# A two-layer decoder on one core: the written-out order of the steps on four engines is replaced, and 111 filler matmuls become 101

## What is computed

```python
x = _layernorm(x + _L0_attn_ref(x, ...))        # 7-wide windowed attention, 16 heads
x = _layernorm(x + _L0_xattn_ref(x, ctx, ...))  # attention to a context
x = _layernorm(x + _L0_ffn_ref(x, ...))         # 8 experts, 16 tokens each, own attention
x = _layernorm(x + _L1_attn_ref(x, ...))        # attention with a decay mask
x = _layernorm(x + _L1_xattn_ref(x, ctx, ...))  # argmax picks a context row, then 16 heads
x = _layernorm(x + _L1_ffn_ref(x, ...))         # ternary weights, 3-wide conv, silu, 1024 hidden
```

## Time and profile before

| | us |
|---|---|
| median of 3 runs | 997.79 (997.18 to 1002.22) |
| the profiled execution, its own time | 997.79 |
| its span | 996.0 |
| PE busy | 924.0 (93%) |
| DVE busy | 855.2 (86%) |
| ACT busy | 737.9 (74%) |
| POOL busy | 217.8 (22%) |

### The profile page before, as it was taken

One profiled execution on the slowest core, in us unless ns is written; L12 is line 12 of the kernel. 1 busy time (PEld: TensorE's weight loads), 2 busy tenths in 40 slices (PEclk: granted clock), 3 DMA queues, 4 the chain that ended last, 5 costly groups with the idle time before them and its releaser, 6 DMA issues.

```text
span 996.0 us, 20555 instructions
## 1 busy us (share of the span) xinstructions
PE 924.0 (93%) x7507; PEld 675.5 (68%) x7507; DVE 855.2 (86%) x2217; ACT 737.9 (74%) x1852; POOL 217.8 (22%) x469
## 2 busy tenths in 40 slices
PE   6888999999999999999999999999999999988887
...
DVE  5887576599999999999999999989999997877877
...
GB/s 277 374 94 74 85 30 66 11 86 1 61 57 62 55 13 105 19 99 1 117 1 44 74 22 96 12 106 2 116 2 43 64 23 1 22 12 12 12 1 22
DMA packets 36629, 59.08 MB, mean 59 GB/s; under 512 B 6656, under 2 KB 15872, under 8 KB 36016
## 3 DMA queue, kind: packets, MB, share of 16 engines
...
## 4 chain that ended last, share of the span: by engine, by line
PE 61%; ACT 16%; DVE 14%; POOL 4%; issue 3%; SPq 2%; DMA 1%; POOLq 0%; DVEq 0%; ACTq 0%
PE bank_c L505 17%; PE banks_e L505 8%; PE bank_a L505 7%; PE bank_x L505 7%; PE bank_f L505 4%; PE bank_x L716 4%; ACT area_e L1768 3%; DVE neg_top L1364 3%; PE bank_a L611 3%; ACT squares_out L1544 2%; PE banks_e L895 2%; DVE area_f L1442 2%; ACT x L1551 2%; ACT area_bx L1532 2%; PE bank_c L536 2%
## 5 line engine op out<-in xcount | busy, mean ns | idle before, releaser
L1442 DVE SCALAR_TENSOR_TENSOR area_f<-area_f,w_convw 128x254 f32<-128x254 f32 x240 | 104.7, 478 | 6.2 <-ACT area_f L1815 4.4
L1532 ACT ACTIVATE area_bx<-bank_x 128x512 f32<-128x512 f32 (+1 forms) x140 | 68.1, 499 | 23.9 <-PE bank_x L716 7.4
L1364 DVE TENSOR_REDUCE neg_top<-banks_e 128x8 f32<-128x1024 f32 x64 | 76.2, 1219 | 8.4 <-PE banks_e L505 8.1
L1213 DVE TENSOR_TENSOR area_a<-area_a 128x512 f32<-128x512 f32 x112 | 74.5, 683 | 1.0
L1158 DVE TENSOR_TENSOR area_a<-area_a 128x512 f32<-128x512 f32 x112 | 73.3, 683 | 2.4 <-PE bank_a L611 1.4
L1815 ACT ACTIVATE area_f<-area_f,w_convb,w_convw 128x256 f32<-128x256 f32 x120 | 65.4, 596 | 10.1 <-DVE area_f L1433 9.7
L1768 ACT ACTIVATE area_e<-banks_e 128x512 f32<-128x512 f32 x120 | 64.1, 602 | 8.4 <-PE banks_e L895 8.1
L1217 DVE TENSOR_TENSOR area_a<-area_a 128x512 f32<-128x512 f32 x96 | 65.7, 684 | 0.4
L1532 ACT ACTIVATE area_a<-bank_a 128x512 f32<-128x512 f32 (+1 forms) x80 | 44.0, 550 | 20.1 <-PE bank_a L505 14.6
L1532 ACT ACTIVATE area_bx<-bank_c 128x512 f32<-128x512 f32 x64 | 34.4, 537 | 26.8 <-PE bank_c L505 19.5
L1864 POOL TENSOR_TENSOR area_bx<-area_bx,minus 128x2 f32<-128x2 f32 x16 | 13.1, 819 | 180.0 <-ACT area_bx L1557 180.0
...
## 6 DMA issues: line engine op xcount, KB each, us to landing
...
```

What stands on the lines that cost most here:

```text
L1213: made[wi] = own.mark(dve.tensor_tensor(v4, v4, bc(e4[:, :, wi, :], 3, DH), ALU.mult))
L1364: dve.tensor_reduce(top[:, b, r:r + 2, :, 0].rearrange("p r (par c) -> p r c par", c=DC), banks_e[:, r:r + 2, :].rearrange("p r (c par k) ...
L1442: last = dve.scalar_tensor_tensor(c4[:, i, :, dst], h4[:, i, :, src], cwt3[:, 2 * jj + i, k:k + 1], c4[:, i, :, dst], ALU.mult, ALU.add)
L1532: return act.activation(dst, src, ACT.Copy)
```

## The change

`WARM` goes from 111 to 101, and the tables of PE, DVE, ACT and POOL are replaced. SP's table stays. No instruction other than the ten fillers is added or removed, no wait and no buffer is changed; each station's steps keep their order among themselves.

```diff
-WARM = 111
+WARM = 101
...
 ORDER = {
     "PE": (
-        "QQQASASSASBQSQBAQAASDABABSBBQBQXBXASAXQXAXABXBABYBYQBYYYQYBAYAXQCXCABXBXAXBAXBQYCYQCYYYBYCAYCAXBXQDAXDXD"
...
+        "QQQASSAASSBQQBSQAQADSBABASBBQBQXBXASAXQXAXABXBABYBYQBYYQYYBAYAXQCXCABXXBAXBAXBQYCYQCYYBYCAYCAXBXQDAXDXD"
...
     ),
```

More of the change, by code:

```diff
@@ L82 @@
-        "WWFWWWWHWWFWWFWWWWWHWWWWHWHHH"
+        "QQQASSAASSBQQBSAQAADSBABASBBQBQXBXASAXQXAXABXBABYBYQBYYQYYBAYAXQCXCABXXBAXBAXBQYCYQYCYYBYCAYCAXBXQDAXDXD"
+        "XDADXEBABYYEQBYCEBEQECYECEYCYECCAEYTDTDADXQDFAXDFDFABXEFBEXBFAXEBXEBFBYECQCEYCECQHYEYCEYHCYTDYTDXADHDADX"
+        "DFQEFBXFEXFBXBFEBEXFBACEBAYCAEYCQCEQYHEYCHYCEYDTYDTDHXADADXDFQEFBFEBAXBFXBXEFXBEBFAYCEYACQECYCEYQYHCECYD"
+        "EYDHTXDTDAHXADDQEFBFXEFBXBFXAEFBEFCXAACYEBBYECQCEYQYCHYEYECYTHDXTDHXDADADFDFQFXEBFEBXAFBEXBXFBAEBAYCEQCY"
@@ new lines @@
+        "ECYECYHEDHEYCYCYTQTDAHXADXDQFDFDAEXBFEBXFBEXBXBFAEBYEFCEAYCQCYQCYECHYCYDYEXEDHATDTDHDAXDQFEFBFXEFBXBABXF"
+        "BEXEFABECYECAYCYQCYHEYQCYEHCEYTDXTADHDXDADDFEFBFXEBXFBQBXFAEBXFEBAECYACYECYECYQHECYHCEYDQTDYDTXDHDAXDABE"
+        "FQFXEFBXBFEBXAFEBFXBAACECEYQCYECQYEYHCYEYTCTYDAXDHADXDHDQDAEFBFEXFBFXBABEXEFABBXCFEQEYCYECYCHYEYCEYTCYDX"
+        "HQDXTDHADADDFQXEFBFEFBXBABXBEFBEFCXEACAYECYECYYHDECYEHCYTBTYDHXDAXDFADFDFXFEXBEBXBXEBFBEYCCFEYECEYCYXYEY"
+        "CEHCTYHDTDXHDDFFDFXDFXCECXEFCCXFCECEYEDYEEYDYHDYHEYDEYDDHTTECCEFCFFCFEECFCEFDEDDEEDEHDTHDTWEHWWEWFWWFWFW"
@@ new lines @@
+        "CAAAAAAQQQQYCAAXXXXXXXXXXAADDDXYYYEEBBAAYYEEEEEEAAAAAAABAAAAAEEAAAAAACCCEQEYQQQTAAFFFDDDAAXXXXFXXXXXFXEE"
+        "FFEEEFEEEFFFBBFFYAYAYXBAAFFFFAFAEEFFFYAYFFCCAAHHAHAAAACEEAAAAAAYHHHHTQQQQHDDDFFFAXXAXXXXXXXEEFXEFEFFEEEE"
+        "FFFFBBFFFFYYYAABFFFXFYYAAEFAAEFAACFFAACAAHHHAAAACEEAAAHHHHYATAQAHFFFDDDAQQQAXXXXXEEXXFXXEEXEEFEFFEBBFFFF"
+        "XYAAYYBFFFFAAYYFFFFAAAFFEEACACAFFAAAAAACAAAAEHHEHYAHHHQHAQTDDQQDHFAFXAXFXXXXXXXEEXEFEFEEFFEFEFFFBXBFFAAF"
+        "FYYYFFAAFAABFAYYFFEEFCCAFAAAAAAAAHAHAHEAAECAYHHHHATHQQFFQFDDDXXAQXXXXXXXAFEEFFFXEEEEEEFFFFBFBAAFFYFXYYBA"
@@ new lines @@
+        "AFFFFFFYYEEAAAAAAFFCCAAHHHAAAAEAEAAACHHAHHAYTQQHQFAFQFADDXDXXXXXXXXAAEEFXEEEEEEFFFFBBFFFXYYYFFBFFAAFFFFY"
+        "YEEAAAAAFAFCCFFAAAACAAAAAHAYAHHAEEHHQQQHHTDDDQHAFXFFXXXXXXXXEEAFXEFFFEEFBEBEEFFFAAFFXFFYBYYFFFEEFAAYYFFA"
+        "AAAFFCAHCAHHAAAAAAAAACEEAYAHHAHHTQQQQHDDDXFFFXXXXXXXAXEEXFEEEAFFFEFBBEEFFFFFAYAFFBYYFXFFFAAYEYFEFAAAAAFF"
+        "CCAAHAHHHHCAEHHAEAAAAYAAAAQTDDDQQXXQXXXHAFXXFXFXEEAXEFEEEFEEFFBBFXFFFFAAFFBFAAYYYAAFFFAAFAEEAAAYYFFCCFFA"
+        "AAEEAAAACAHHHAAYQTHHHHAAQQQDDDXXFXXXHFXXXAFXEEAEFXEEEFEEFFBBFFFFAAFBFFYYYFFFEEFFFFYYAAAAFXAFCCAAAEEAAAAC"
@@ L101 @@
+        "HYHHAAAAAHHAHHXXQXTXXXHXXDDDFFFXAAQQQEEFEXEFFFFBBEEEEFFFXFBFFAAFFYYYFFFAAFFEEAYYFAFCCAHAAHHAAAEEHHCHHAAA"
+        "ATAAYAAAAHFFFDXDDXXXXXXAXXFXFEEFFXEEFEBEBEEFFYFYYBFFFFFEYEYFFFFFCCFFEEHHHCYHHHHTXXXXXHFFFDDDXXXXFXXFFFEF"
+        "EFEEEEFEEFCCFFFFFYFYYFCFFFYEEYFFHHHHHDEDDHHYETHEEFFFEEEEFEECCFFFFFCFFFFFFFFFFFFFFEEDEDEDHHHHHHHTEEHFFFEE"
+        "EEFEEFFFFFFFFFFFFFFFFFEEFEFEHHHHHTHHFFFHFFFFFFFFFFFFFFFFFFFFHHHHHHHHH"
     ),
     "ACT": (
-        "QQSQSSASSASBQBQASQAADSABSABBSSSSSBQSSBBSXQSXAABQXAXSBXSABBAYSSBYQYYBYBSQYSSBAYAYXQCXACBXBASXABXYQCBYYQYC"
```

57 lines of the change are left out of this document (18 added, 39 removed).

## The result

The changed kernel takes 1013.73 us (median of 4 runs, 1013.01 to 1014.0), the kernel before beside it 999.5 us (997.18 to 1002.22, 4 runs): a ratio of 1.0139, with a 95% interval of 1.0112 to 1.0166. The prediction was 1001.9 us with a range of 989 to 1009. The time lies outside it. The profiled execution of the changed kernel took 1010.35 us, and its span is 1008.4 us: 12.4 more than before, where the sum said 4.1. It is the shortest of the six executions on record and has the highest mean granted clock, 0.991 (the other five took 1012.94 to 1014.0 us at 0.985 to 0.989).

The account below looks back on a forecast made before the run. PE was taken to set the pace, busy 97% from 200 to 850 us. Span 996.0 + 1.0 + 3.9 - 0.8 = 1000.1 us, plus 1.8 around the span, gave 1001.9 us, range 989 to 1009.

Parts of the forecast that it names:

- The end of E15: Last group, on DVE: group 14's convolution and other instructions now stand before and between E15's, sliding its end by +3.9 us.
- The middle: 200 to 850 us: the new order taken as nothing, bounded by 10 us of gain and 6 us of loss.
- neighbours of one bank: PE's table, middle: two steps of one bank with nothing between, 12 before and 13 now, 0.5 us each on average.
- the middle gets worse: Rival, PE from 200 to 850 us: ten or twelve more short waits, +5 to +6 us, 1007 us; chance 0.14.
- D15's queries: On ACT near the end: the copy `chosen_q` starts later behind more exponentials and a copy, +1.0 us.
- H14 out of the last stretch: On DVE, 966 to 987 us: H14's addition moves in front of F15's first L1433, -0.8 us.
- Fillers: Last stretch on PE: ten fillers fewer cost nothing, as they stand where PE would be waiting anyway.
- The clock rival: Last stretch: fewer fillers let PE's clock fall in H15's pairs, 1.4 us later, 1003.3 us; chance 0.12.

Follow-up runs that it names:

- part4: The kernel before with the new order only from T14's addition (934 us) to the end, 101 fillers; ratio 1.0054 to the kernel before.
- tail_old: The changed kernel up to T14, from there the old order with its 111 fillers; ratio 1.0098 to the kernel before, span 1005.1 us.
- swaps: The changed kernel with another step put between adjacent steps of one chain, on PE alone, in five places from 834 to 917 us; ratio 1.024 to the kernel before.
- part3b: The kernel before with the new order only from X14's addition (847 us) to T14 (934 us); ratio 1.0025 to the kernel before, span 998.7 us.
- few_fillers: The kernel before with 22 fillers fewer behind F15's first step, 89 in all; ratio 1.0021 to the kernel before, span 998.8 us.
- act_d15: The changed kernel with D15's copy of the queries moved ahead of an L1824 and E14's copy, on ACT alone; ratio 1.0133 to the kernel before.

## Why the prediction was wrong, and where it was right

**The end of E15, +3.9: right in size and in mechanism.** The change makes 3.8 us between T14 and E15's addition; putting the new tail on the old front makes 3.8 too (part4), and putting the old tail on the new front takes it to 0.1 (tail_old).

**The middle, taken as nothing: the step that failed most.** Up to C13 the change loses 6.2 us, of them 2.5 by 758 us and 3.7 in the 87 us behind it. The prediction counted neighbours of one bank, 12 before and 13 now, at 0.5 us each, and found the difference too small to matter. The count was a sample of one cause of waits, and it was taken over the whole middle in one piece. By lines of the table it goes from 11 to 8 in the second to seventh and from 1 to 5 in the eighth, and the eighth, by its steps in the trace, covers about 745 to 850 us (the ninth what follows, not "800 to 900"). There the waits grew by five, and by 2.3 us, and those for ACT by 3.0. So the rise was in the tables, in the place where the time was lost. The rival "the middle gets worse" named the right place, PE waiting for copies, and its 5 to 6 us is nearly what came. Its price per wait is not confirmed: the stretch is 4.0 us longer with 2.3 us more of waits, and swaps, which took such pairs apart, only made others. Which letters do it I have not separated, so the cause inside the stretch stays open; that it is the order and not the clock, the traces show. (The prediction also took all of PE's idle time in the middle for waits for copies. Of its recorded waits there before, 18.7 us, 4.5 are for DVE.)

**From 850 to 934 us: a stretch that was left out of the sum.** The prediction took one detail from it, D15's queries, for +1.0, and treated it with the letters beside it. It is 2.4 us in the change and 2.6 alone (part3b), and 4.5 alone when the old order too has its full clock there. The detail was exact, 3.98 us between the two copies, and the sentence that went with it was wrong: the two L1815 "cost nothing as long as that idle time is there". It was not there, and in the old order it is there only where the clock falls. ACT in part4, with the old order at a granted clock of 1.00:

```profile
921.05 0.57 ACT L1532 ACTIVATE area_d<-bank_c 128x512 f32<-128x512 f32 x1
```

No idle time stands ahead of the copy; there PE waits 0.72 us for it. The 1.83 us of rows 4 are ACT waiting for PE's transposes, behind logits and a product that ran at half clock (2.02 us for 1.09). An idle time is a cover only if what makes it will be there again.

**H14 out of the last stretch, -0.8: 0.6 in part4, nothing in the change.** From the first L1433 to L1501 the kernel before takes 15.92 us, part4 with the new tail 15.35, so it gains 0.6. The changed kernel takes 15.89: at half clock the transposes at L977 take 1.06 to 1.11 us for 0.6, and DVE waits 0.59 for the last of them. It may be no gain of its own either: in the old order H14's L1511 come only behind E15's addition, so it seems to be E15's delay that makes room for it. No run tests that.

**Fillers, nothing: right where they only fill, wrong as a cover.** The clock rival, of 1.4 us in H15's product, came in part4 (1.3), few_fillers (1.1), act_d15 (1.8) and swaps (1.3), and in the change as the 0.5 us of the step above. The Trainium skill ("TensorE: Matmul & The Clock Gate", its section on a second HAM failure mode) says that many short idle times between groups of matmuls make the clock swing. These runs agree: PE is idle for 5.1 and 5.6 of the 21 us ahead of the product in few_fillers and part4 and for 2.3 in the kernel before, which has a clock of 1.00 up to 987 us and pairs 0.22 us apart in the product. The five slower executions of the change may have lost their 2.6 to 3.7 us in this way; none of them has a trace.

Together: the sum had 4.1 us and the span grew by 12.4. Of the missing 8.3, 7.6 lie ahead of T14 and 0.7 behind it. The median is a further 3.4 us above the profiled execution. The range gave the middle 6 us of loss, and with the other terms that ends near 1009; the profiled execution, at 1010.35, is just past it, and the range had nothing for the two places and the clock together. The direction was right, and the sum had a third of the loss.
